# Four graph layers on one core: pair 0 split while x is multiplied, sweep 5's steps at other places, layer 1's result kept in O

## The reference, cut to what matters

```python
x = layernorm(x + L0(x))  # L0: tanh MLP of x, plus adj @ XB - rowsum(adj) * XB, XB = x @ B.T
x = layernorm(x + L1(x))  # Chebyshev: three products with adj in turn, each times its own 64x64 weights
x = layernorm(x + L2(x))  # [x, (adj @ x + x) / deg] @ W + b, relu, rows brought to length 1
x = layernorm(x + L3(x))  # decay weights 0.5**rank from the position of the nonzeros in each row
```

## Time and profile before

| what | value |
|---|---|
| median of 3 runs | 3085.93 us (3082.61 to 3086.66) |
| profiled execution, its own time | 3082.01 us |
| span of that profile | 3080.2 us |
| mean granted PE clock | 0.992 of full |
| PE, PEld busy | 95%, 70% |
| DVE busy | 92% |
| ACT busy | 76% |
| DMA engines' mean busy share of q1 | 94.6% |

### The profile page before, as it was taken

How to read it: one execution, slowest core, us unless ns; L and a number is a source line. 1 busy time by engine, 2 the same in 40 slices (tenths; PEclk the granted TensorE clock), 3 DMA queues, 4 the chain that set the end, 5 groups by cost and what they waited for, 6 DMA issues and landing times.

```text
span 3080.2 us, 35223 instructions
## 1 busy us (share of the span) xinstructions
PE 2934.1 (95%) x13425; PEld 2164.8 (70%) x13488; DVE 2831.4 (92%) x2407; ACT 2353.7 (76%) x1619; POOL 13.2 (0%) x31
## 2 busy tenths in 40 slices
PE   7999999999999998999989999998889999999998
PEld 6767778787788886888867888776766555555554
DVE  7999988988998889988899988999999999999997
ACT  5787877777777678776777776877777888888887
POOL 0000000000000000000000000000000000000000
PEclk9999999999999999999999999999999999999999
DMA  9999988999999999999999999989999999999996
GB/s 339 388 395 382 387 352 343 369 361 359 370 394 382 377 374 399 387 386 378 377 369 374 382 375 379 377 328 349 373 405 405 359 385 385 377 389 377 388 386 251
DMA packets 159015, 1148.18 MB, mean 373 GB/s; under 512 B 18160, under 2 KB 18336, under 8 KB 19584
## 3 DMA queue, kind: packets, MB, share of 16 engines
q1 hardware_dynamic: 157312, 1143.02, 94.6%
q0 software_dynamic: 1088, 2.48, 0.2%
q10 hardware_dynamic: 448, 0.43, 0.0%
HBM read 1143.75 MB, written 2.10 MB: 372 GB/s over the span
## 4 chain that ended last, share of the span: by engine, by line
PE 66%; DVE 23%; DMA 5%; ACT 3%; issue 2%; ACTq 0%; DVEq 0%
PE ACC L887 26%; DVE lo L626 17%; PE ACC L894 15%; PE ACC L1003 14%; DMA raw<-in_at 5%; PE PST L1017 4%; PE PSF L1017 3%; ACT hi L444 2%; PE PST L910 1%; DVE SV L737 1%; PE PSF L960 1%; DVE M L641 1%; PE PSF L967 0%; PE PSF L983 0%; PE PSF L963 0%
## 5 line engine op out<-in xcount | busy, mean ns | idle before, releaser
L626 DVE TENSOR_TENSOR lo<-raw,hi 128x2048 fp32r<-128x2048 f32 x832 | 1876.4, 2287 | 140.0 <-ACT hi L444 136.2
L444 ACT CAST hi<-raw 128x2048 fp32r<-128x2048 f32 x832 | 1584.7, 1912 | 526.2 <-PE ACC L887 338.4
L887 PE MATMUL ACC<-hi,T 128*128 128x512 f32 x4992 | 1280.6, 393 | 4.5 <-ACT hi L444 2.8
L887 PEld LDWEIGHTS ACC<-hi,T 128*128 128x128 f32 x4992 | 936.0, 189 | 207.6 <-issue 3.9
L894 PE MATMUL ACC<-lo,T 128*128 128x512 f32 x3200 | 887.4, 399 | 103.4 <-DVE lo L626 96.9
L894 PEld LDWEIGHTS ACC<-lo,T 128*128 128x128 f32 x3200 | 589.5, 189 | 298.4 <-DVE lo L626 183.9
L641 DVE SCALAR_TENSOR_TENSOR M<-raw,M 128x512 bf16<-128x512 f32 x1008 | 637.1, 687 | 40.9 <-PE ACC L1003 24.2
L450 ACT ACTIVATE Wf<-ACC,w_bias 128x1024 fp32r<-128x1024 f32 x512 | 568.1, 1114 | 128.5 <-PE ACC L1003 127.9
L1003 PE MATMUL ACC<-M,rank_b 128*128 128x512 bf16 x1969 | 518.3, 382 | 12.2 <-ACT Wf L450 6.7
L1003 PEld LDWEIGHTS ACC<-M,rank_b 128*128 128x128 bf16 x2032 | 158.8, 98 | 266.5 <-issue 131.2
L1017 PE MATMUL PST<-Wf,S 128*128 128x512 f32 x512 | 209.3, 489 | 0.0
(11 more groups left out here) (156 smaller groups left out, 1004.8 us busy)
## 6 DMA issues: line engine op xcount, KB each, us to landing
raw<-in_at SPq DMA_DIRECT2D x1088, 1024.0 KB, 6.8
SV<-in_x_cols SPq DMA_DIRECT2D x8, 256.0 KB, 10.1
out<-O POOLq DMA_DIRECT2D x7, 256.0 KB, 6.9
out<-O ACTq DMA_DIRECT2D x1, 256.0 KB, 2.0
w_sb<-in_w POOLq DMA_DIRECT2D x3, 64.0 KB, 9.6
bias<-in_bias_rows ACTq DMA_DIRECT2D x1, 128.0 KB, 11.8
l1w_sb<-in_l_w POOLq DMA_DIRECT2D x2, 64.0 KB, 8.4
rank_f<-in_rank_mats POOLq DMA_DIRECT2D x1, 128.0 KB, 10.2
```

What stands on the lines that cost most here:

```text
L444: nc.scalar.copy(hi[:, c % NH], raw[:, c % NR]).then_inc(hi_done, 1)
L626: tt(lo[:, c % NR], raw[:, c % NR], hi[:, c % NH].bitcast(f32), ALU.subtract).then_inc(lo_done, 1)
L887: ins = mm(acc[:, part], w, hi[:, p.c % NH, s, part], start=p.opens and s == 0 and i == 0, stop=False)
```

## The change

1. `b_t` is laid out as one array of 64 x 128 with the centring matrix beside it, so `cx` comes with one DMA.
2. Pair 0's `split_hi` stands ahead of `high_part(0)` on ACT, and its `split_lo` ahead of the first operand's parts on DVE. `first_operand` is cut in two, `operand_parts` and `x_itself`, with the same operations in the same order.
3. Sweep 4's `fin_b` writes the normalised result to `O` instead of `xr`. In sweep 5 `whole` is gone; `tpx` transposes `O`, and `fin_b1` adds `O`.
4. In sweep 5, rows 1 to 6: `tpx` and `tx` two pairs earlier; rows 0 to 6: `relu`, its `root`, `s_hi` and `s_lo` one pair earlier.

```diff
         elif r < NB - 1:
-            due("DVE", c - 3, "whole", k, r)
-            due("PE", c - 2, "tpx", k, r)
-            due("ACT", c + 1, "tx", k, r)
+            early = 2 if r else 0
+            due("PE", c - 2 - early, "tpx", k, r)
+            due("ACT", c + 1 - early, "tx", k, r)
...
-            due("ACT", c + 8, "relu", k, r)
+            due("ACT", c + 7, "relu", k, r)
             due("DVE", c + 7, "length", k, r)
-            due("ACT", c + 9, "root", k, r)
+            due("ACT", c + 8, "root", k, r)
...
-            due("ACT", c + 22, "s_hi", k, r)
-            due("DVE", c + 21, "s_lo", k, r)
+            due("ACT", c + 21, "s_hi", k, r)
+            due("DVE", c + 20, "s_lo", k, r)
         else:
-            due("DVE", c - 3, "whole", k, r)
             due("PE", c - 2, "tpx", k, r)
...
-            act.dma_start(cx[:, 0:D], b_t).then_inc(c_cx, 16)
-            act.dma_start(cx[:, D:2 * D], centre).then_inc(c_cx, 16)
+            act.dma_start(cx[:], b_t).then_inc(c_cx, 16)
...
+            split_hi(0)
             high_part(0)
             for c in range(n_all):
                 if c < n_pairs:
-                    split_hi(c)
+                    if c:
+                        split_hi(c)
...
             def fin_b(k, I):
-                ins = scale()
+
+                dst = xr[:] if k == 1 else O[:, gs(I), :]
+                ins = scale(dst)
...
-                write_v(k, I, xr[:]).then_inc(v_done, 1)
+                write_v(k, I, dst).then_inc(v_done, 1)
...
-                    link(tt(xr[:], xr[:], xo[:], ALU.add))
+                    link(tt(xr[:], xr[:], O[:, g, :], ALU.add))
...
-            first_operand(0)
+            split_lo(0)
+            operand_parts(0)
+            x_itself(0)
...
-                    pe.wait_ge(xo_done, r + 1)
+                    pe.wait_ge(v_done, v_count[4, I])
                     pst_free(what, r)
-                    transpose(PST, xo).then_inc(tpx_done, 1)
+                    transpose(PST, O[:, gs(I), :]).then_inc(tpx_done, 1)
```

More of the change, by code:

```diff
@@ L37, in graph_layers @@
 def graph_layers(nc, at, x_cols, t_col, b_t, w1, w1_t, b1_c, w2, bias_rows, l1_w, l2_w, l3_w,
-                 ident, rank_mats, centre, pick, out):
+                 ident, rank_mats, pick, out):
     f32, f32r, bf16 = mybir.dt.float32, mybir.dt.float32r, mybir.dt.bfloat16
@@ L139, in graph_layers @@
     x_done, tp_done, tt_done, w_done = sem("x_done"), sem("tp_done"), sem("tt_done"), sem("w_done")
-    xo_done, tpx_done, tx_done = sem("xo_done"), sem("tpx_done"), sem("tx_done")
+    tpx_done, tx_done = sem("tpx_done"), sem("tx_done")
     var_ready, sd_ready = sem("var_ready"), sem("sd_ready")
@@ L346, in graph_layers @@
     psf_put = {key: n + xb0 for key, n in psf_put.items()}
-    tps, whole_no = numbered("PE", "tp"), numbered("DVE", "whole")
+    tps = numbered("PE", "tp")
     pst_turn = numbered("PE", "tp", "tpx")
@@ L580, in over_rows, with operand_parts @@
                 return row.unsqueeze(1).broadcast_to([P, Q, D])
-            def first_operand(b):
-                I = block_of(1, b, NB)
-                g, most = gs(I), slice(0, D - 1)
+            def operand_parts(b):
+                g, most = gs(block_of(1, b, NB)), slice(0, D - 1)
                 dve.wait_ge(th_done, b + 1)
@@ L587, in first_operand, with x_itself @@
                 copy(T[:, g, 0, 1, most], T[:, g, 1, 0, most].bitcast(f32)).then_inc(t_init, 1)
+            def x_itself(b):
+                g = gs(block_of(1, b, NB))
                 copy(RD[:, g], PSF[:, :, D - 1])
@@ L661, in rooted, with scale @@
                 dve.wait_ge(sd_ready, roots[0])
-            def scale():
+            def scale(dst):
                 rooted()
                 link(nc.vector.reciprocal(st3[:], st2[:]))
-                return tt(xr[:], xr[:], over_feats(st3[:]), ALU.mult)
+                return tt(dst, xr[:], over_feats(st3[:]), ALU.mult)
             def write_v(k, I, src):
@@ L718, in step @@
                 elif what == "t_init":
-                    first_operand(r)
+                    operand_parts(r)
+                    x_itself(r)
                 elif what == "x_lo":
@@ L746, in step @@
                 elif what == "whole":
[L747 to L753, removed]
+                    dve.wait_ge(v_done, v_count[1, I])
+                    src = T[:, g, :, 1].bitcast(f32)
+                    link(tt(xo[:], src[:, :, 0], src[:, :, 1], ALU.add))
                 elif what == "fin_a":
@@ L772, in step @@
                 elif what == "fin_c":
-                    scale().then_inc(x_done, 1)
+                    scale(xr[:]).then_inc(x_done, 1)
                 elif what == "res":
@@ L820, in out_scale @@
                 tt(O[:, gs(I), :], O[:, gs(I), :], over_feats(RD[:, gs(I)]), ALU.mult).then_inc(out_ready, 1)
-            dve.wait_ge(c_cx, 32)
+            dve.wait_ge(c_cx, 16)
             link(nc.vector.tensor_reduce(st1[0:D, 0:1], cx[:, 0:D], AX, ALU.add))
@@ L825, in _ @@
                 cx_ready, 1)
-            first_operand(0)
+            split_lo(0)
+            operand_parts(0)
+            x_itself(0)
             for c in range(n_all):
                 if c < n_pairs:
-                    split_lo(c)
+                    if c:
+                        split_lo(c)
                 else:
@@ L1049 @@
 _INS = ["at", "x_cols", "t_col", "b_t", "w1", "w1_t", "b1_c", "w2", "bias_rows", "l1_w", "l2_w",
-        "l3_w", "ident", "rank_mats", "centre", "pick"]
+        "l3_w", "ident", "rank_mats", "pick"]
 def lay_out(x, adj, L0_gnn_t, L0_gnn_B, L0_gnn_W1, L0_gnn_b1, L0_gnn_W2, L0_gnn_b2, L1_gnn_weights,
@@ L1075, in lay_out @@
         "t_col": c(np.broadcast_to(np.asarray(L0_gnn_t).reshape(1, 1), (P, HID // P))),
-        "b_t": c(np.asarray(L0_gnn_B).T),
+        "b_t": c(np.concatenate([np.asarray(L0_gnn_B).T, np.eye(D, dtype=np.float32) - np.float32(1 / D)], 1)),
         "w1": c(w1[:D]),
@@ L1087, in lay_out @@
         "rank_mats": c(np.stack([later, 1 - later], 1)),
-        "centre": np.eye(D, dtype=np.float32) - np.float32(1 / D),
         "pick": pick,
```

## The result

| | before | changed |
|---|---|---|
| median, 7 runs each | 3082.65 us | 3074.01 us |
| lowest to highest | 3079.53 to 3086.66 | 3070.34 to 3076.59 |
| ratio, 95% interval | | 0.9969 (0.9959 to 0.9979) |
| span of the profiled execution | 3080.2 us | 3071.8 us |

The changed kernel is faster by 0.31%, or 9.6 us by the ratio (8.6 by the medians). The forecast was 3075 with a gain of 10.6. The size is right. Of its parts three were priced too low or too high by more than a us, as the experiments show.

What follows compares the result with a forecast made beforehand. DVE was taken to bound sweep 5's dense part, DVE and loads in turn from 2162. Terms 1.2 + 4.0 + 2.7 + 0.6 + 2.1 = 10.6 us took the median from 3085.9 to 3075.3, said as 3075; range 3067 to 3084.

Steps and rivals of the forecast that it cites:

- its first reading: In the dense part of sweep 5, 1990 to 2103 us, DVE binds, and a us taken from it shortens the end.
- start: At the kernel's start, one DMA fewer and pair 0 split first: refill issued 3.9 us earlier, of which 1.2 is kept.
- One sign of being right: Sweep 5, row 0's to row 4's `fin_a`: some 7 us shorter, its loads well above 336 GB/s.
- `whole` gone: Sweep 5: dropping DVE's eight `whole` steps saves 0.61 us each, half of that behind 2162; 4.0 us in all.
- `relu` early: Sweep 5: `relu` a pair earlier ends `length`'s waits for ACT's squares, less an allowance for late `hi`; 2.7 us.
- `tpx` and `tx` early: Sweep 5: two pairs earlier, PE's passes fill idle time and `lo` no longer waits for a late `hi`; 0.6 us.
- `s_hi`, `s_lo` early: Sweep 5: a pair earlier, they remove 2.1 us of `s_lo`'s 4.2 us of waits in four rows.
- the gap of 1.3: At the start: second refill lands 3.8 us after the first, where 1 MB takes 2.5; 1.3 us to be closed.
- The allowance of 0.3 a row: In `relu`'s term, sweep 5: 0.3 us a row set aside for a `hi` that is late instead.
- the wait for `S` at 2151: `s_lo`'s 2.12 us wait in sweep 5; with `tpx` gone from between, most goes, 1.6 us.
- The new neighbour: Row 4's `tpx` at pair 63 must wait for row 3's `tt`; hardly a wait, 1 us once, in PE's slack.
- The clock: PE in sweep 5: half speed follows the wait, so multiplications would take it; transposes' gain, 1.7 us a row, not counted.

Runs made afterwards that it cites:

- e5: The changed kernel with `relu`, `root`, `s_hi` and `s_lo` back at their old places, only `tpx` and `tx` early; ratio to the kernel before 0.9981.
- e12: The changed kernel with `tpx` and `tx` alone back at their old places, `relu`, `s_hi` and `s_lo` early; ratio to the kernel before 0.9970.
- e3: The changed kernel with all of sweep 5's steps at their old places, new start and result in `O` kept; ratio to the kernel before 0.9981.
- e1: The kernel before with only the new start (one DMA for `cx`, pair 0 split first); ratio to the kernel before 0.9993 (0.9984 to 1.0002).
- e6: The changed kernel with `tpx`, `tx`, `s_hi` and `s_lo` back at their old places, only `relu` and `root` early; ratio to the kernel before 0.9962.
- e10: The changed kernel with `tpx`, `tx` and `s_lo` back at their old places, `relu`, `root` and `s_hi` early; ratio to the kernel before 0.9961.

## Why the prediction was right, and where its parts were not

The time came out as forecast, within 1 us of 3075, and its first reading holds: in the dense part of sweep 5 DVE is the bound, and most of what DVE doesn't do comes off the end. The nearness of the time is partly luck. It was reckoned from a median of 3085.9, and the kernel before has 3082.65 over seven runs; from there the forecast's gain gives 3072.0. The gain of 10.6 was measured as 9.6, with an interval from 6.5 to 12.6. Within it errors cancel: the start and `relu` were priced too low, `s_lo` too high. One sign of being right failed: row 0's to row 4's `fin_a` was to be some 7 us shorter and is 3.6, and the loads in it went from 336 only to 342 GB/s.

The terms, as measured:

| term | forecast | measured |
|---|---|---|
| start | 1.2 | 1.4 by the profiles at 60 us; 2.6 (standard error 0.6) by the times |
| `whole` gone | 4.0 | 3.5 |
| `relu` early | 2.7 | 4.2 alone |
| `tpx` and `tx` early | 0.6 | 0.3 alone, -0.3 beside relu (less than B can tell) |
| `s_hi`, `s_lo` early | 2.1 | 0 alone, -1.0 beside relu (less than B can tell) |
| the three moves together | 5.4 | 3.2 |

The parts seen in sweep 5 make 6.7 us, 3.5 and 3.2, and with the start's 2.6 the sum is 9.3, beside 9.6 by the ratio.

- **Start.** The refill at 17.4 was right (17.56), and so was the landing near 30.7. The second landed 1.4 earlier, as the gap of 1.3 said. The third landed at 37.0 in both, so the queue didn't keep the gap closed. But the landing is not what counts there: the kernel before took that load only at 39.05. The 1.2 was a choice between nothing and 3.9. That 1.4 are left at 60 us speaks for it, and the times say that it was too low.
- **`whole`.** The mechanism was right. The price of 0.61 a row came for row 0, and about 0.4 a row for rows 1 to 4, since part of it turned into waits for `hi`.
- **`relu`.** The allowance of 0.3 a row for a late `hi` was too much, though the sum took it for four rows where it had six. And I had not seen that `relu` early also takes 1.2 of the wait for `S` at 2151.
- **`s_lo`.** This is the step that was wrong: "with `tpx` gone from between, most of that goes". With `tpx` alone early (e5) the wait at 2151 goes from 2.12 only to 1.67. It did shrink to 1.02 in the changed kernel, but `relu` alone brings it to 0.9. And with one `lo` less as a cover, beside an early `relu`, the other rows came to wait: 3.2 us in four rows with `relu` alone, 4.2 in seven with `s` added (e12), 4.3, 3.0 and 3.7 in six or seven with all moves.
- **Waits counted twice.** The 2.12 us was a price in one term only, but three of the edits each shorten it, by 0.4 to 1.2. And some 1 us of waits for `hi` between rows 1 and 3, which arose when `whole` went and stood in no row of the kernel before, is removed by `tpx` and by `s` alike. The worth of moves taken one by one is too high by what they share.
- **The new neighbour**, `tpx` behind `tt` at row 4, was foreseen with a wait of hardly anything to 1 us; it was 0.72. That it would lie in PE's slack was wrong: PE's delay went on to ACT's `hi` and DVE, 0.99.
- **The clock.** Behind the wait for a late `lo` the multiplications would run at half speed in place of the transposes, I said. The half speed did leave the transposes. The longest transpose of `O` took 477 ns with the old places (e3) and 323 in the changed kernel:

```profile
L913 PE MATMUL PST<-eye,O x128: 272/273/477, 1971.4 to 2343.7; 128*64 128x128 f32 x128
```

```profile
L914 PE MATMUL PST<-eye,O x128: 272/273/323, 1970.5 to 2340.7; 128*64 128x128 f32 x128
```

From row 0's to row 4's `fin_a`, 25 of e3's 128 transposes took over 400 ns, and none in any of the six profiles with an early `tpx`. It went only in part to the multiplications: their time above 389 ns each, their median, is 6.4 us in e3 and 7.2 in e5, with `tpx` alone early, while the transposes' half speed had cost some 5. The granted clock of the dense part is 0.95 in e3 and 1.00 in e5, 0.94 in the kernel before and 0.98 in the changed one. Little of it shows in B (0.3 for `tpx` alone), since PE isn't the bound there.

What stays open: how much of the start's gain is kept and where (e1 alone holds anything from 4.9 us faster to 0.6 slower; the three pairs together say 2.6), what `tpx` and `s` are worth behind row 4, where B tells no less than 1.2 us, and whether e6 or e10 is really better than the changed kernel.

## What to carry to other kernels

Before adding up several small edits, list for each the waits that it removes, those that an earlier edit of the same set creates included, and count a wait once; two edits that each cure the same wait are worth one. On strictly ordered engines a step that waits is helped by an earlier producer and not by its own earlier place: `s_hi` alone removed every wait for `S` that `s_hi` and `s_lo` together had left, and was faster (e10 against e12). And an issue that comes earlier but lands no earlier can still leave a lead, where the old kernel took the load after its landing: look at when the engine takes it. A lead of a few us at the start of a long kernel is lost in the spread of single profiles; pairs of kernels that differ by it alone, timed beside each other, show it.

## What was not expected of the hardware

Two profiles of one and the same kernel reached row 0's `fin_a` at 1986.94 and 1991.93, and e12's at 1994.23, while from there to row 4's `fin_a` such profiles agree within 0.2 us. Most of the spread arises in sweep 1 (the last of the eight `XS` copies started at 682.0 and 686.7); why is not shown. The stretch in which DVE binds repeats. So parts of a change that work there are told apart at 0.2 us, where the interval of a ratio is some 3 us to either side.
